# Slot softmax's division carried into the RMS factor of a fused transformer layer, with the gated output rewritten

## The reference, cut to what matters

```python
s  = clip(hs @ Ws1.T @ Ws2.T + bs2, -32, 32)             # per head: [T, 64]
z  = cumlogsumexp(s, axis=time); es = exp(s); enz = exp(-z)
A  = where(mask, rope(q) @ rope(k).T * scale, 0)
ok = enz * (A @ es)
qv = softmax(ok, axis=-1)                                # over the 64 slots
W2 = where(mask, (qv * enz) @ es.T, 0)
o  = W2 @ v
o_n = o * rsqrt(mean(o * o) + EPS) * g_norm_weight       # per token and head
o_g = o_n * (g * sigmoid(g)); out = o_g @ Wo.T
```

## Time and profile before

| | us |
|---|---|
| median of 3 runs | 920.13 |
| lowest, highest | 918.7, 923.7 |
| span of the profiled execution | 922.5 |
| TensorE busy in the span | 817.4 |
| VectorE busy | 683.4 |
| ScalarE busy | 482.6 |
| GpSimd busy | 292.7 |

### The profile page before, as it was taken

The page is one execution under the profiler, slowest core; times in us unless marked ns, Lnnn a source line. Parts: engine busy times, 40 slices in busy tenths (PEclk is TensorE's granted clock), DMA queues, the critical chain, the costliest instruction groups (busy, mean ns, idle before and its releaser), DMA issues.

```text
span 922.5 us, 14194 instructions
## 1 busy us (share of the span) xinstructions
PE 817.4 (89%) x4428; PEld 687.2 (74%) x4428; DVE 683.4 (74%) x1500; ACT 482.6 (52%) x1280; POOL 292.7 (32%) x287
## 2 busy tenths in 40 slices
PE   3999999999999846998998998998989989989963
PEld 2788888888888734876887787787778768767852
DVE  6455545454545688698889889888888988987876
ACT  3455555465455325565574664755656655555420
POOL 7011011010010145244344353362452553442222
PEclk9999999999999979998999999998999999989997
DMA  7011010110110010001001001001000010000001
GB/s 223 1 46 40 5 45 0 45 45 0 45 63 5 1 58 1 1 12 47 0 11 45 0 11 45 11 0 46 11 27 18 11 45 0 11 0 0 1 1 45
DMA packets 23653, 23.74 MB, mean 26 GB/s; under 512 B 2369, under 2 KB 23361, under 8 KB 23506
## 3 DMA queue, kind: packets, MB, share of 16 engines
q1 hardware_dynamic: 23634, 23.51, 8.1%
HBM read 22.45 MB, written 1.05 MB: 25 GB/s over the span
## 4 chain that ended last, share of the span: by engine, by line
PE 61%; POOL 12%; issue 10%; DVE 9%; ACT 6%; DMA 1%; POOLq 0%; ACTq 0%; SPq 0%; DVEq 0%
PE ps L1202 12%; PE ps L1396 9%; PE ps L1207 6%; PE ps L1230 4%; PE ps L1309 4%; POOL rot_s L417 4%; PE ps L1457 4%; PE ps L1273 3%; ACT wv L710 2%; PE ps L1249 2%; DVE xn L777 2%; POOL wc_lo L358 2%; DVE qp L1018 2%; PE ps L1314 2%; POOL qp L436 2%
## 5 line engine op out<-in xcount | busy, mean ns | idle before, releaser
L358 POOL TENSOR_TENSOR w_lo<-w_raw,w_hi 128x512 fp32r<-128x512 f32 x32 | 43.7, 1378 | 218.0 <-ACT w_hi L501 218.0
L1202 PE MATMUL ps<-xT_hi,w_hi 128*128 128x512 f32 x256 | 110.0, 430 | 3.1 <-DVE xT_lo L784 1.9
L1202 PE MATMUL ps<-xT_hi,w_lo 128*128 128x512 f32 x256 | 101.5, 397 | 0.0
L417 POOL TENSOR_TENSOR rot_s<-rot_s,const 128x512 f32<-128x512 f32 x64 | 89.4, 1408 | 38.0 <-ACT rot_s L637 38.0
L1202 PE MATMUL ps<-xT_lo,w_hi 128*128 128x512 f32 x256 | 100.9, 394 | 0.0
L957 DVE TENSOR_TENSOR rot<-rot,const 128x512 f32<-128x512 f32 x64 | 74.1, 1158 | 28.7 <-ACT rot_s L637 28.7
L987 DVE TENSOR_TENSOR wt<-ps,const 128x384 f32<-128x384 f32 x128 | 68.2, 550 | 10.8 <-PE ps L1458 8.1
L545 ACT ACTIVATE wt<-wt,negmax 128x128 f32<-128x128 f32 (+1 forms) x128 | 56.6, 444 | 36.1 <-DVE negmax L853 36.1
L841 DVE TENSOR_TENSOR v<-ps,bv_b 128x256 f32<-128x256 f32 x64 | 26.9, 422 | 59.5 <-PE ps L1207 59.4
L1207 PE MATMUL ps<-wv,xT 128*128 128x256 f32 x256 | 63.1, 380 | 1.0 <-DVE v L841 1.0
L1396 PE MATMUL ps<-wc_hi,xT_hi 128*128 128x512 f32 x128 | 60.6, 473 | 1.3 <-ACT rot_s L637 0.7
(11 more groups left out here) (158 smaller groups left out, 2327.8 us busy)
## 6 DMA issues: line engine op xcount, KB each, us to landing
w_raw<-a_w_q SPq DMA_DIRECT2D x8, 256.0 KB, 3.4
w_raw<-a_w_k SPq DMA_DIRECT2D x8, 256.0 KB, 3.8
wv<-a_w_v SPq DMA_DIRECT2D x8, 256.0 KB, 2.5
wo<-a_w_o SPq DMA_DIRECT2D x8, 256.0 KB, 3.3
w_raw<-b_Wq SPq DMA_DIRECT2D x8, 256.0 KB, 2.6
w_raw<-b_Wk SPq DMA_DIRECT2D x8, 256.0 KB, 3.4
wc<-b_Wv SPq DMA_DIRECT2D x8, 256.0 KB, 3.5
wc<-b_Wg SPq DMA_DIRECT2D x8, 256.0 KB, 3.9
```

Source lines behind the costliest of these rows:

```text
L358: g.tensor_tensor(lo[:, :, :], raw[:, :, :], hi[:, :, :].bitcast(F32), ALU.subtract).then_inc(ph.w_lo, 1)
L417: g.tensor_tensor(ap, ap, const[:, col:col + T].unsqueeze(1).to_broadcast([P, 2, T]), ALU.mult).then_inc(b_rotmul, 1)
L1202: ins = mm(PJ[n[0]], w[:, m, c, h * P:(h + 1) * P], x[:, c, cols], start=(t == 0), stop=(t == len(terms) - 1))
```

## The change

- The slot softmax is no longer divided by its sum. `slots` on GpSimd makes qp directly. VectorE computes okeps = (oksum * EPS) * oksum in place of the reciprocal, and `rms` on GpSimd adds okeps where it added a constant; it waits for okeps in addition to oss.
- The gated output is made by four `scalar_tensor_tensor` instructions of 128 columns, each (o * factor) * gate with o from PSUM, the factor one column of orms and the gate from SBUF, in place of two `tensor_tensor` of 512 columns. They wait for orms; before, the first product waited for oss. The scores' masks, which in turns 0 and 2 stood between the two products, now stand ahead of the output in every turn.
- The product ok = enz * (A @ es) is one instruction for both heads, through an access pattern written by hand.
- The memset of the constant goes, and two waits count one less.

```diff
-            g.memset(eps4[:, :], RMS_EPS).then_inc(init_done, 1)
...
             def rms(x):
                 pool.wait_ge(b_oss, x + 1)
-                g.tensor_tensor(oms[:, :], oss[:, :], eps4[:, :], ALU.add).then_inc(b_oms, 1)
+                pool.wait_ge(b_okeps, x + 1)
+                g.tensor_tensor(oms[:, :], oss[:, :], okeps[:, :], ALU.add).then_inc(b_oms, 1)
...
                 g.tensor_tensor(qp[:, :, :], oke[:, :, :, :].rearrange("p t h m -> p t (h m)"),
-                                enz[:, 2 * b:2 * b + 2, :], ALU.mult).then_inc(b_qp1, 1)
+                                enz[:, 2 * b:2 * b + 2, :], ALU.mult).then_inc(b_qp, 1)
...
-                for h in range(2):
-                    ins = d.tensor_tensor(ok[:, :, h, :], X_[0].rearrange("p (h t m) -> p h t m", h=2, t=2)[:, h, :, h * M:(h + 1) * M],
-                                          enz[:, 2 * b:2 * b + 2, h * M:(h + 1) * M], ALU.mult)
-                ins.then_inc(b_okn, 1)
+                own = bass.AP(X_[0].tensor, X_[0].offset, [X_[0].ap[0], [P, 2], [T + M, 2], [1, M]])
+                d.tensor_tensor(ok[:, :, :, :], own, enz[:, 2 * b:2 * b + 2, :].rearrange("p t (h m) -> p t h m", h=2),
+                                ALU.mult).then_inc(b_okn, 1)
...
                 dve.wait_ge(b_oksum, x + 1)
-                d.reciprocal(okinv[:, :], oksum[:, :]).then_inc(b_okinv, 1)
-                dve.wait_ge(b_qp1, x + 1)
-                dve.wait_ge(b_okinv, x + 1)
-                ap = qp[:, :, :].rearrange("p t (h m) -> p (t h) m", h=2)
-                d.tensor_tensor(ap, ap, okinv[:, :].unsqueeze(2).to_broadcast([P, 4, M]), ALU.mult).then_inc(b_qp, 1)
+                d.scalar_tensor_tensor(out=okeps[:, :], in0=oksum[:, :], scalar=RMS_EPS, in1=oksum[:, :],
+                                       op0=ALU.mult, op1=ALU.mult).then_inc(b_okeps, 1)
...
-                    if nxt and not first:
+                    if nxt:
                         b_scores(x + b + 1)
-                    dve.wait_ge(b_oss, x + b + 1)
-                    d.tensor_tensor(og[:, :], O_, G[:, 2 * b:2 * b + 2, :].rearrange("p t n -> p (t n)"), ALU.mult
-                                    ).then_inc(b_og0, 1)
-                    if nxt and first:
-                        b_scores(x + b + 1)
                     dve.wait_ge(b_orms, x + b + 1)
-                    dve.wait_ge(b_og0, x + b + 1)
-                    d.tensor_tensor(og[:, :].rearrange("p (a n) -> p a n", a=4), og[:, :].rearrange("p (a n) -> p a n", a=4),
-                                    orms[:, :].unsqueeze(2).to_broadcast([P, 4, P]), ALU.mult).then_inc(b_og, 1)
+                    for k in range(4):
+                        cols = slice(k * P, (k + 1) * P)
+                        ins = d.scalar_tensor_tensor(out=og[:, cols], in0=O_[:, cols], scalar=orms[:, k:k + 1],
+                                                     in1=G[:, 2 * b + k // 2, (k % 2) * P:(k % 2 + 1) * P],
+                                                     op0=ALU.mult, op1=ALU.mult)
+                    ins.then_inc(b_og, 1)
```

More of the change, by code:

```diff
@@ L150, in layer_kernel @@
         oksum = sb("oksum", [P, 4])
-        okinv = sb("okinv", [P, 4])
         qp = sb("qp", [P, 2, 2 * M])
@@ L157, in layer_kernel @@
         oms = sb("oms", [P, 4])
-        eps4 = sb("eps4", [P, 4])
+        okeps = sb("okeps", [P, 4])
         orms = sb("orms", [P, 4])
@@ L229, in layer_kernel @@
         a_masked, a_max, a_exp, a_rinv, a_norm, a_pt_ps, a_pt = (sem("a_" + n) for n in ("masked", "max", "exp", "rinv", "norm", "pt_ps", "pt"))
-        (b_es, b_es_hi, b_es_lo, b_sums, b_rotmul, b_rotcos, b_recip_done, b_rope, b_sc, b_okps, b_okn, b_okmax, b_oksub, b_okexp, b_oksum, b_okinv, b_qp1,
-         b_qp, b_qt_ps, b_z, b_w2_ps, b_w2, b_oss, b_oms, b_orms, b_og0, b_og, b_ogt_ps, b_gt,
+        (b_es, b_es_hi, b_es_lo, b_sums, b_rotmul, b_rotcos, b_recip_done, b_rope, b_sc, b_okps, b_okn, b_okmax, b_oksub, b_okexp, b_oksum, b_okeps,
+         b_qp, b_qt_ps, b_z, b_w2_ps, b_w2, b_oss, b_oms, b_orms, b_og, b_ogt_ps, b_gt,
          b_wos) = (sem("b_" + n) for n in (
-             "es", "es_hi", "es_lo", "sums", "rotmul", "rotcos", "recip", "rope", "sc", "okps", "okn", "okmax", "oksub", "okexp", "oksum", "okinv",
-             "qp1", "qp", "qt_ps", "z", "w2_ps", "w2", "oss", "oms", "orms", "og0", "og", "ogt_ps",
+             "es", "es_hi", "es_lo", "sums", "rotmul", "rotcos", "recip", "rope", "sc", "okps", "okn", "okmax", "oksub", "okexp", "oksum", "okeps",
+             "qp", "qt_ps", "z", "w2_ps", "w2", "oss", "oms", "orms", "og", "ogt_ps",
              "gt", "wos"))
@@ L296, in _ @@
             sp.dma_start(gw[:, :], b_gw.rearrange("(p o) -> p o", o=1)).then_inc(small_ld, 16)
-            sp.wait_ge(init_done, 5)
+            sp.wait_ge(init_done, 4)
             sp.dma_start(ws2[0:RANK, :], b_ws2).then_inc(small_ld, 16)
@@ L734, in b_body @@
                         ffn_copy(1, 0)
-            act.wait_ge(init_done, 5)
+            act.wait_ge(init_done, 4)
             act.wait_ge(gwh_done, 1)
```

## The result

| | us |
|---|---|
| after: median, lowest, highest of 4 runs | 908.16, 901.62, 911.19 |
| before: median of 4 runs in the same comparison | 919.91 |
| ratio, 95% interval | 0.984, 0.981 to 0.987 |
| span of the profiled execution (its own time 908.63) | 906.8 |

The change makes the kernel faster by 12 to 15 us, depending on whether medians or the ratio are read. A second comparison gave 907.8 against 922.78, ratio 0.985 (0.982 to 0.987). The forecast was 904, with 892 to 916 as its range.

What follows compares the result with a forecast made beforehand. TensorE was taken as the bound, with gains only from its stalls before qp's transposes: 1.90 us a pair, x7 = 13.3, plus tail 1.4, lead-in 0.2 and clock 1.4, in all 16.3, giving 904 us; range 892 to 916.

Steps and rivals of the forecast that it cites:

- the sum of a pair, 1.90: TensorE's stalls before qp's transposes: 0.97 in turn 2, 0.35 in turn 0, 0.58 in turn 1, 1.90 us a pair.
- the 0.59 that the masks were to take back: Stall of turn 1: VectorE's score masks become the late thing, leaving 0.35 us of the 0.94 by which qp comes earlier.
- Output, 1.14 us from one row of another shape: Gated output on VectorE: four 128-wide instructions take 1.14 us in all, estimated from a row of two 256-wide ones.
- Rival D: Output on VectorE: the four new instructions wait for GpSimd on the shared port; 21 us slower, 941; chance 0.08.
- Turn 2, 0.97: VectorE and GpSimd in turn 2: qp comes earlier, so the 3.47 us stall of turn 3 shrinks by 0.97, to 2.5.
- rival C: Shared port after the output: another grant order, rotary sum before GpSimd's second product, eats the gain; 9.3 us won, 911; chance 0.17.
- Turn 0, 0.94 earlier: Turn 0, before the stall of turn 1: qp comes 0.39 + 0.07 + 0.48 = 0.94 us earlier.
- Turn 3, nothing: Turn 3: no stall to win, the output just in time for TensorE; costed at 0, perhaps 0.05 us lost.
- Clock, 1.4 won: TensorE's clock behind turn 3's stall: with the shorter stall one of the doubled low stretches goes, 1.4 us won.
- Rival B: TensorE's clock in turn 3: it stays up behind a 2.5 us stall; 8.8 us more won, 895; chance 0.15.
- Tail and last pair, 1.4: Eighth pair's tail: masks before the product 0.5, L1018 gone 0.42 + 0.05, shorter output 0.4; together 1.4 us won.
- The 0.2 of the lead-in turn: The lead-in turn: 0.2 us won.

Runs made afterwards that it cites:

- kernel before, copies early: Kernel before the change, with ScalarE's rotary copies of k0 in turns 0 and 2 moved ahead of the slots' exp: one run, 938.06 us against 923.7.
- ok product alone: Kernel before the change, with only both heads' ok product made in one instruction: one run, 918.47 us (median of before 922.71).
- output alone: Kernel before the change, with only the four-instruction output and its order, the division staying: 912.83 us against 922.78, ratio 0.989.
- division alone: Kernel before the change, with only the softmax division carried into the factor, output and ok products staying: 916.82 us against 922.78, ratio 0.993.
- with copies early: Changed kernel with ScalarE's rotary copies of k0 ahead of the slots' exp, GpSimd's weight tail staying in place: one run, 893.23 us.
- masks behind the output: Changed kernel with the scores' masks of turns 0 and 2 moved behind the four output instructions: one run, 913.5 us.

## Why the prediction came out as it did

The mechanism was right in turns 0 and 2, and the result lies 4 us from the forecast; the sum of a pair, 1.90, was measured as 1.89. But its split over the turns was partly wrong, two errors cancelled, and that the sum fits so closely is luck: with the 0.59 that the masks were to take back booked in turn 1, that turn won 0.45 more than forecast, and turn 3 lost 0.51 that was put at nothing.

- *Output, 1.14 us from one row of another shape*: 1.12 measured, 0.26 apart, 341 to 352 ns each, beside GpSimd's long products too. Rival D is excluded: a scalar operand from SBUF does not bring these instructions to the shared port. The Trainium skill ("SBUF — State Buffer", section "SBUF: two separate sides") names the VectorE instructions that take the shared port pair: those in a two-port mode, and those with two SBUF inputs against a GpSimd instruction that reads SBUF. The trace agrees, with these 341 to 352 ns for instructions whose one tensor from SBUF is the gate.
- *Turn 2, 0.97*: 1.01. The stall itself only fell to 2.74, not 2.5, because TensorE gets there 0.27 earlier: it comes to og's projection 12.16 behind the turn's transposes and not 12.43. The order on the port was as forecast (second rotary product, rotary sum, weight tail, product), so rival C did not come.
- *Turn 0, 0.94 earlier*: 0.95, with the same effect on the stall: 0.55 is left, not 0.3, as og's projection starts 0.24 earlier. That TensorE runs back to back outside its stalls was not quite so.
- *What is late next in turn 1*: the failing step. I let VectorE's masks before L1473 take back 0.59 of that 0.94. VectorE does end the masks in time (652.15, with L1466 at 652.27); what was late is the first projection behind qp's transposes, L1389, for whose bank it waits until ScalarE has copied. I had looked at ScalarE for z0 and not at the bank that the same copies set free. L1466 starts 5.15 behind the transposes where L1473 started at 4.70, so the bank takes back 0.45 in turn 1, 0.14 less than forecast. The rest of turn 1's gain beyond the forecast is again TensorE's way behind that: og's transposes come 0.13 sooner behind the products A @ es, and the stretch from og's projection to turn 2's transposes is 2.06 and not 2.80, where the stall explains 0.58.
- *Turn 3, nothing*: it became 0.51 longer, nearly all by the same bank (0.46 up to the product with v). "No stall to win" was true, but its start had moved to where the next thing was not ready. og itself was in time there, as forecast.
- *Clock, 1.4 won*: this is the mis-sized term. A stall of 2.74 us is followed by no low stretch, one of 3.4 or one of 6.8, and it differs between executions: against a turn 3 with the clock up, the low stretches of the profiled execution cost 12.6 us, those of the second one 4.6, those of before 10.6: 2.0 lost in one execution and 6.0 won in the other, where 1.4 won was forecast. Most of the range of 901.6 to 911.2 is this term, as far as two traces can show. Rival B came true in three pairs of seven in one execution. The Trainium skill ("TensorE: Matmul & The Clock Gate", section "HAM oscillation — how this bites in real kernels") says long idle gaps bring the throttle back; the traces agree at the ends and not in between. By the length of the stall, in how many of the seven pairs a low stretch followed:

| stall, us | where | pairs of seven |
|---|---|---|
| 4.51 | kernel before, copies early, turn 3 | 7 |
| 3.47 | kernel before, turn 3 | 7 |
| 3.40 | ok product alone, turn 3 | 7 |
| 3.27 | output alone, turn 3 | 6 |
| 3.02 | division alone, turn 3 | 7 |
| 2.74 | change, turn 3, in two executions; with copies early | 7, 4; 5 |
| 2.31 | kernel before, copies early, turn 1 | 0 |
| 1.88 | masks behind the output, turn 0; turn 2 | 5; 1 |
| 1.28 or less | every kernel | 0 |

So the length of the one stall doesn't decide it: 1.88 had a low stretch behind it more often than 2.31.
- *Tail and last pair, 1.4*: 1.3. The 0.2 of the lead-in turn can't be told apart from the start's 3 us of clock.

Not settled: what decides whether a low stretch follows a stall of 1.9 to 3.3 us and how long it is, and why some executions have 3.4 or 6.8 us more of half clock before the first turn than others.

## What to carry to other kernels

When a stall shrinks, list everything that the next few instructions of the waiting engine need, buffers to be freed included; the one you leave out is where the gain goes. In these kernels two SBUF operands on VectorE beside GpSimd were paid in whole instructions, so count whose turn it is, and take the long GpSimd instruction out of the stretch before anything else: moving one by a few lines won 26 us here where three rewrites of VectorE's work won 12 to 15. And the same move can win or lose by what stands beside it: try it again after each change. Add up all turns of a pair before judging a move: what one turn loses, the next can win back.

## What the runs showed of the hardware that I had not expected

- The small multiply that replaced the reciprocal (128x4) takes 307 to 339 ns, the reciprocal 178. No TensorE wait ends at it here.
- With one program, TensorE's granted clock fell to half behind the same 2.74 us stall in some pairs and not in others, and the seven turns 3 of the two traced executions differ by 8.0 us by that alone.
